# The second expert layer of a perceiver kernel: token and expert pairs sorted into 23 tiles of 128 slots, instead of every expert run over all 1024 tokens

## The reference

```python
probs = softmax(einsum('bsd,ed->bse', x, router_w))
token_probs, probs_idx = top_k(probs, 2)
gates = sum(token_probs[..., None] * one_hot(probs_idx, 8), axis=-2)
# for each expert e:
y = gelu(x @ wg_w[e].T + wg_b[e], approximate=False)     # 256 -> 1024
h = y * (x @ w1_w[e].T + w1_b[e])                        # 256 -> 1024
out = h @ w2_w[e].T + w2_b[e]                            # 1024 -> 256
acc = acc + out * g[..., None]
```

## Time and profile before

| | |
|---|---|
| median of 3 runs | 5568.69 us (5562.72 to 5574.45) |
| profiled execution, its own time | 5562.66 us |
| its span in the trace | 5560.9 us |
| mean granted TensorE clock | 0.912 of full |
| `l1_ffn`, first load to its last DVE instruction | 3040.4 to 3622.4 us |

### The profile page before, as it was taken

How to read it: one execution, slowest core, us unless ns; L and a number is a source line. 1 busy time by engine, 2 the same in 40 slices (tenths; PEclk the granted TensorE clock), 3 DMA queues, 4 the chain that set the end, 5 groups by cost and what they waited for, 6 DMA issues and landing times. The chain is left out here.

```text
span 5560.9 us, 113654 instructions
## 1 busy us (share of the span) xinstructions
PE 4837.1 (87%) x45694; PEld 3720.1 (67%) x45694; DVE 3035.0 (55%) x5687; ACT 2118.8 (38%) x4053; POOL 935.9 (17%) x473
## 2 busy tenths in 40 slices
PE   6879999998759989999766899987689989998877
PEld 4659888896549966666423788876269956665465
DVE  5358777772554455555287433354633366664443
ACT  1235555552134434444243333343034434443121
POOL 0022222220002200000076122142612200000200
PEclk8889999999669999999988899988879999999885
DMA  1010000000101111110022111022911010000110
GB/s 60 29 36 15 15 22 15 16 7 27 50 31 45 45 43 50 38 50 26 22 76 69 46 45 50 18 81 57 121 46 53 23 38 26 27 21 33 42 59 30
DMA packets 195844, 222.91 MB, mean 40 GB/s; under 512 B 43251, under 2 KB 164932, under 8 KB 187236
## 3 DMA queue, kind: packets, MB, share of 16 engines
q1 hardware_dynamic: 195428, 216.93, 13.9%
HBM read 170.09 MB, written 15.34 MB: 33 GB/s over the span
## 5 line engine op out<-in xcount | busy, mean ns | idle before, releaser
L2367 DVE TENSOR_REDUCE block_max<-PS 128x1 f32<-128x512 f32 (+1 forms) x896 | 505.5, 627 | 300.3 <-PE PS L2227 299.7
L2316 ACT ACTIVATE probs_turned<-PS 128x512 f32<-128x512 f32 (+1 forms) x896 | 434.6, 571 | 563.3 <-PE PS L2248 563.2
L1632 PE MATMUL PS<-input_part,part_up 128*128 128x512 f32 x2304 | 552.5, 393 | 18.4 <-DVEq L1713 8.6
L1645 PEld LDWEIGHTS PS<-part_down,hidden_part 128*128 128x128 f32 x4608 | 548.7, 189 | 2.0
L1645 PE MATMUL PS<-part_down,hidden_part 128*128 128x256 f32 x4608 | 549.1, 281 | 0.0
L1685 ACT ACTIVATE hidden<-PS,b 128x512 f32<-128x512 f32 x384 | 264.4, 689 | 651.7 <-PE PS L1632 637.2
L1632 PEld LDWEIGHTS PS<-input_part,part_up 128*128 128x128 f32 x2304 | 434.9, 190 | 110.1 <-DVEq L1713 9.3
L844 PE MATMUL PS<-context_turned,queries 128*128 128x512 f32 x1728 | 413.4, 384 | 25.3 <-issue 18.4
L876 PE MATMUL PS<-probs_turned,context_part 128*128 128x256 f32 (+2 forms) x3120 | 410.1, 286 | 3.7 <-DVE weighted L953 3.7
L905 ACT CAST probs_turned<-PS 128x512 fp32r<-128x512 f32 x576 | 261.2, 510 | 358.3 <-PE PS L856 358.3
L1721 DVE TENSOR_TENSOR hidden_part<-hidden,hidden_part 128x512 fp32r<-128x512 f32 x384 | 293.8, 774 | 183.1 <-ACT hidden_part L1675 182.4
(11 more groups left out here) (441 smaller groups left out, 8052.8 us busy)
## 6 DMA issues: line engine op xcount, KB each, us to landing
context_rows<-in_ctx SPq DMA_DIRECT2D x40, 768.0 KB
raw_up<-in_L_ffn_W SPq DMA_DIRECT2D x16, 1024.0 KB, 4.8
raw_down<-in_L_ffn_W SPq DMA_DIRECT2D x16, 1024.0 KB, 4.8
v_all<-v_turned SPq DMA_DIRECT2D x128, 128.0 KB, 19.4
ctx_turned<-context_turned SPq DMA_DIRECT2D x16, 800.5 KB, 4.7
context_turned<-ctx_turned SPq DMA_DIRECT2D x16, 800.5 KB
b_all<-bc_turned SPq DMA_DIRECT2D x32, 256.0 KB, 3.5
c_all<-bc_turned SPq DMA_DIRECT2D x32, 256.0 KB, 4.3
```

The costliest lines, as they stand in the source:

```text
L1632: last = nc.tensor.matmul(PS[:, k % ring + 2 * x, :], bank.parts[name][a][:, c, f * P:(f + 1) * P], h[b][:, c, half * 512:(half + 1) * 512 ...
L1645: last = nc.tensor.matmul(PS[:, 4 + t % outs, 0:DIM], aT[a][:, f, t * P:(t + 1) * P], bank.parts["down"][b][:, f, :], start=(f == 0 and m ...
L2316: nc.scalar.activation(probs[0:kk, t % ring, i, 0:many].rearrange("p k c s -> p (k c s)"), PS[0:kk, bank_of("turned", t, i), 0:many * 2 * ...
L2367: nc.vector.tensor_reduce(part[:, b % 2, chunks[0]:chunks[-1] + 1, i, u // 2], bank, AX_X, ALU.max).then_inc(max_done.sem, 1)
```

## The change

`l1_ffn` no longer calls `gate_bias` and `experts`, but `routed_experts`. The 1024 tokens have 2048 pairs (token, chosen expert). The pairs of an expert get consecutive slots, and each expert begins at a multiple of 128 slots, so that a tile of 128 slots belongs to one expert; 23 tiles (`SLOTS`) hold any distribution, and all 23 are always computed. DVE works out each pair's slot (`idx`) and each tile's expert (`expert_of`) from `first` and `second`, with two small PE matmuls for the counts. GpSimd scatters the rows of U into a tensor in device memory, `slot_rows`, with 16 indirect transfers of 128 rows, and SP loads all slots back in four batches. For each tile, SP reads the expert's number into a register and loads that expert's three weight tensors (1 MB each) and two columns of biases into one of three buffers. PE turns a tile's rows over, multiplies, and the sums of each tile are stored to `slot_sums` in device memory by ACT's queue. At the end GpSimd gathers the two sums of every token with 16 indirect transfers, and DVE adds them, times the token's two probabilities, to X. The output biases are weighted with the gates as before, but added to X before the tiles. The matmuls are on float32 itself: no operand is split. Before the tiles are scattered, `slot_rows` is filled from the input x (three transfers of 1, 1 and 0.9 MB) so that unused slots hold numbers.

```diff
+SLOTS = 2 * TOKENS // P + EXPERTS - 1
...
+class RoutedExperts:
...
+        self.ring = 3
+        sizes = {"up": [P, self.ring, DC, 4 * DIM], "second": [P, self.ring, DC, 4 * DIM], "down": [P, self.ring, 4 * DC, DIM]}
...
+        self.slot_rows = core.nc.dram_tensor(name, (SLOTS * P, DIM), F32, kind="Internal").ap()
...
+        x, cuts = d["x"], range(0, SLOTS * P, TOKENS)
+        self.loads = [(self.slot_rows[r:min(r + TOKENS, SLOTS * P)], x[0:min(TOKENS, SLOTS * P - r)], self.filled) for r in cuts]
...
+def routed_experts(core, bank, rows, first, second, share, b2, iota, func, skip=None):
...
+    x_bank, y_bank, small_bank = 4, 5, 7
...
+    batches = [range(n, min(n + 6, SLOTS)) for n in range(0, SLOTS, 6)]
...
+                def weights_of(i):
+                    u = i % ring
+                    e = sp.value_load(expert_of[0:1, i:i + 1], min_val=0, max_val=EXPERTS - 1)
+                    if i >= ring:
+                        sp.wait_ge(up_ready.sem, up_ready.at((i - ring + 1) * GROUPS))
+                    for k in up_names:
+                        sp.dma_start(bank.w[k][:, u], bank.source[k][bass.ds(e, 1)].squeeze(0)).then_inc(w_landed[k][u].sem, 16)
+                    if i >= ring:
+                        sp.wait_ge(made.sem, made.at((i - ring + 1) * FC))
+                    for k, src in bank.columns.items():
+                        sp.dma_start(bank.col[k][:, u], src[bass.ds(e, 1)].squeeze(0)).then_inc(c_landed[u].sem, 16)
+                    if i >= ring:
+                        sp.wait_ge(y_ready.sem, y_ready.at(i - ring + 1))
+                    sp.dma_start(bank.w["down"][:, u], bank.source["down"][bass.ds(e, 1)].squeeze(0)).then_inc(w_landed["down"][u].sem, 16)
+                sp.wait_ge(tile_ready.sem, tile_ready.at(1))
+                weights_of(0)
+                sp.wait_ge(scattered.sem, scattered.at(16 * 2 * TILES))
+                for n, some in enumerate(batches):
+                    sp.dma_start(xg[:, some[0]:some[-1] + 1, :],
+                                 bank.slot_rows[some[0] * P:(some[-1] + 1) * P].rearrange("(i p) d -> p i d", p=P)).then_inc(brought[n].sem, 16)
+                for i in range(1, SLOTS):
+                    weights_of(i)
...
+                pool.wait_ge(bank.filled.sem, bank.filled.past)
+                pool.wait_ge(place_ready.sem, place_ready.at(1))
+                for t in range(TILES):
+                    for k in range(2):
+                        nc.gpsimd.indirect_dma_start(bank.slot_rows, bass.IndirectOffsetOnAxis(idx[:, k, t:t + 1], 0), rows[:, t, :],
+                                                     None).then_inc(scattered.sem, 16)
+                for k in range(3):
+                    pool.wait_ge(stored[k].sem, stored[k].at(16 * len(range(k, SLOTS, 3))))
+                for t in range(TILES):
+                    for k in range(2):
+                        nc.gpsimd.indirect_dma_start(yk[:, k, t, :], None, bank.slot_sums,
+                                                     bass.IndirectOffsetOnAxis(idx[:, k, t:t + 1], 0)).then_inc(gathered[t // 2].sem, 16)
...
+                then(v.memset(ones[:], 1.0))
+                then(v.tensor_tensor_scan(below[:], ones[:], core.ident[:], 0.0, ALU.mult, ALU.add))
+                v.tensor_tensor(below[:], below[:], core.ident[:], ALU.subtract).then_inc(ones_made.sem, 1)
+                v.tensor_tensor(both[:], first[:], second[:], ALU.add).then_inc(counted.sem, 1)
...
+                dve.wait_ge(prefix.sem, prefix.at(1))
+                then(v.tensor_copy(tot[:].rearrange("p e t -> p t e"), PS[:, small_bank, 64:128].rearrange("p (t e) -> p t e", e=EXPERTS)))
+                then(v.tensor_tensor_scan(flat(cum), flat(fresh), flat(tot), 0.0, ALU.mult, ALU.add))
...
+                v.tensor_copy(idx[:], at2[:]).then_inc(place_ready.sem, 1)
...
+                v.tensor_copy(expert_of[:], expert[:]).then_inc(tile_ready.sem, 1)
...
+                for n, b in enumerate((2, 3, 5, 6)):
+                    tiles = X[:, 2 * n:2 * n + 2, :]
+                    v.tensor_tensor(tiles, PS[:, b, :].rearrange("p (t d) -> p t d", d=DIM), tiles, ALU.add).then_inc(bias_taken.sem, 1)
...
+                for i in range(SLOTS + 1):
+                    if mult and i < SLOTS:
+                        dve.wait_ge(c_landed[i % ring].sem, c_landed[i % ring].at(16 * len(bank.columns) * (i // ring + 1)))
+                        for f in range(FC):
+                            dve.wait_ge(up_act.sem, up_act.at(i * FC + f + 1))
+                            v.scalar_tensor_tensor(hT[:, i % 2, f, :], PS[:, 2 + f // 4, (f % 4) * P:(f % 4 + 1) * P],
+                                                   bank.col["second"][:, i % ring, f:f + 1], a32[:, i % 2, f, :],
+                                                   ALU.add, ALU.mult).then_inc(h_ready.sem, 1)
+                    if i:
+                        dve.wait_ge(y_ready.sem, y_ready.at(i))
+                        if i > 3:
+                            dve.wait_ge(stored[(i - 1) % 3].sem, stored[(i - 1) % 3].at(16 * ((i - 1) // 3)))
+                        v.tensor_copy(ysb[:, (i - 1) % 3, :], PS[:, y_bank + (i - 1) % 2, 0:DIM]).then_inc(y_moved.sem, 1)
+                dve.wait_ge(bias_taken.sem, bias_taken.at(4))
+                for t in range(TILES):
+                    for k in range(2):
+                        n = t * 2 + k
+                        dve.wait_ge(gathered[t // 2].sem, gathered[t // 2].at(64))
+                        if k:
+                            dve.wait_ge(summed.sem, summed.at(n))
+                        v.scalar_tensor_tensor(X[:, t, :], yk[:, k, t, :], share[:, t, k:k + 1], X[:, t, :],
+                                               ALU.mult, ALU.add).then_inc(summed.sem, 1)
...
+                def turned_out(i):
+                    act.wait_ge(x_ready.sem, x_ready.at(i + 1))
...
+                def sums_out(i):
+                    act.wait_ge(y_moved.sem, y_moved.at(i + 1))
+                    act.dma_start(bank.slot_sums[i * P:(i + 1) * P], ysb[:, i % 3, :]).then_inc(stored[i % 3].sem, 16)
+                turned_out(0)
+                for i in range(SLOTS):
+                    act.wait_ge(c_landed[i % ring].sem, c_landed[i % ring].at(16 * len(bank.columns) * (i // ring + 1)))
+                    if mult and i >= 2:
+                        act.wait_ge(h_ready.sem, h_ready.at((i - 1) * FC))
+                    for f in range(FC):
+                        if f % 4 == 0:
+                            act.wait_ge(up_ready.sem, up_ready.at(i * GROUPS + f // 4 + 1))
+                        nc.scalar.activation(a32[:, i % 2, f, :], PS[:, f // 4, (f % 4) * P:(f % 4 + 1) * P], func,
+                                             bias=bank.col["up"][:, i % ring, f:f + 1]).then_inc(up_act.sem, 1)
+                    if i + 1 < SLOTS:
+                        turned_out(i + 1)
+                    if i >= 2:
+                        sums_out(i - 2)
...
+                last.then_inc(bias_ready.sem, 1)
+                def turned(i):
+                    pe.wait_ge(brought[i // 6].sem, brought[i // 6].at(16))
+                    if i:
+                        pe.wait_ge(x_taken.sem, x_taken.at(DC * i))
+                    for c in range(DC):
+                        last = nc.tensor.transpose(PS[:, x_bank, c * P:(c + 1) * P], xg[:, i, c * P:(c + 1) * P], core.ident[:])
+                    last.then_inc(x_ready.sem, 1)
+                def up(i):
+                    u = i % ring
+                    pe.wait_ge(x_taken.sem, x_taken.at(DC * (i + 1)))
+                    for k in up_names:
+                        pe.wait_ge(w_landed[k][u].sem, w_landed[k][u].at(16 * (i // ring + 1)))
+                    for f in range(FC):
+                        if i and f % 4 == 0:
+                            pe.wait_ge(made.sem, made.at((i - 1) * FC + f + 4))
+                        for x, k in enumerate(up_names):
+                            for c in range(DC):
+                                last = nc.tensor.matmul(PS[:, 2 * x + f // 4, (f % 4) * P:(f % 4 + 1) * P],
+                                                        bank.w[k][:, u, c, f * P:(f + 1) * P], xT[:, i % 2, c, :],
+                                                        start=(c == 0), stop=(c == DC - 1))
+                        if f % 4 == 3:
+                            last.then_inc(up_ready.sem, 1)
+                def down(i):
+                    u = i % ring
+                    pe.wait_ge(w_landed["down"][u].sem, w_landed["down"][u].at(16 * (i // ring + 1)))
+                    pe.wait_ge(made.sem, made.at((i + 1) * FC))
+                    if i >= 2:
+                        pe.wait_ge(y_moved.sem, y_moved.at(i - 1))
+                    for f in range(FC):
+                        last = nc.tensor.matmul(PS[:, y_bank + i % 2, 0:DIM], hT[:, i % 2, f, :], bank.w["down"][:, u, f, :],
```

(36 more changed lines are left out.)

164 lines of the change are left out of this document (added).

## The result

The changed kernel takes 5299.65 us (median of 4 runs, 5285.47 to 5301.34) against 5570.66 us for the kernel before, run beside it (5562.72 to 5574.45): a ratio of 0.951, with a 95% interval of 0.949 to 0.9529.

The account below looks back on a forecast made before the run. TensorE's matmul time was taken to bound the expert loop (busy 532.0 of 533.0 us). Way in, 23 tiles at 11.5 us (265) and way out made 361.6 us instead of 582.0, leaving 5342, plus 6: 5348 us; range 5315 to 5455.

Parts of the forecast that it names:

- two best experts known: Start of the sublayer: 26.6 us less 2 for a dropped bias load the router waited for, 24.6 (bounds 23 and 31).
- 16 scatters and landing: Before the tiles: 16 indirect transfers on GpSimd at 1.5 us each, 24 us, then 2.0 us for the landing.
- lower clock, second tile: Start of the tile loop: PE begins at half clock and the second tile's weights queue behind slot loads, 4 us for both.
- way out: After the tiles: copy, issue and landing, 16 gathers at 1.5 us, landing, last additions: 31 us.
- Of the profiled execution's 5562.7 us 5342 remain: Whole program: the stage's 220 us saving taken off the profiled execution, every other sublayer keeping its time.
- I take 0.119 x 64 = 7.6 us: Up matmuls of a tile: 64 float32 passes of 128 columns at 0.119 us each, 7.6 us.
- four waits of 0.05 us a tile: PE in each tile: four waits already met, estimated at 0.05 us each, 0.2 us together.
- Rival 1: Tile matmuls: weight loads and short float32 streams don't overlap, up to 141 us more, 5489 us; chance 0.07.
- Rival 2: Scatters and gathers: indirect transfers cost nearer 4.86 us each, 107 us more, 5455; chance 0.10 for over 3 us.
- Rival 3: Tile loop: PE's clock stays at 0.50, a tile takes 22.8 us, 259 us more, 5607, slower; chance 0.05.
- Rival 4: GpSimd: each indirect transfer holds the queue until landed, 19.4 us, 573 us more, 5921, slower; chance 0.03.
- The sum by non-overlapping transfers: Scatters and gathers: at the skill's 2.3 us per transfer without overlap, 32 x 0.8 = 26 us higher, 5374 us.

Follow-up runs that it names:

- run 1: The kernel after, again, with no edit: 5302.04 us against 5560.47 for the kernel before, ratio 0.9546; sublayer 335.5 us.
- run 2: The kernel before, again, with no edit: 5568.15 us; sublayer 582.0 us.
- run 5: The kernel after with up matmuls that stream 64 columns instead of 128: sublayer 348.4 us, 12.9 more; a pass still 0.1115 us.
- run 11: The kernel after with half the weight columns in all up matmuls: sublayer 338.4 us, 2.9 more; four passes every 0.437 us.
- run 6: The kernel after with only the first choice's eight gathers and additions at the end: sublayer 324.5 us, 11.0 less; whole 5318.35 us.
- run 3: The kernel after with each weight load moving half its weights, used twice by the matmuls: sublayer 335.5 us, unchanged; whole 5292.99 us.
- run 7: The kernel after with the weights of the first three tiles, not one, issued before SP waits for the scatters: sublayer 344.5 us, 9.0 more.
- run 12: The kernel after with only the first choices' eight scatters: sublayer 328.6 us, 6.9 less.
- run 14: The kernel after with twelve small dependent DVE steps added behind the sublayer: sublayer 338.5 us, 3.0 more; whole 5310.9 us.
- run 4: The kernel after with two buffers for each weight tensor instead of three: sublayer 348.6 us, 13.1 more.
- run 9: The kernel after with half the weight columns in every second group of up matmuls, streams whole: sublayer 396.5 us, 61 more.
- run 10: The kernel after with half the weight columns and half the streamed columns in every second group of up matmuls: sublayer 359.9 us.
- run 13: The kernel after with fifty small dependent DVE steps added behind the sublayer: sublayer 346.2 us, 10.6 more; whole 5341.57 us.

## Why the prediction missed low

Inside the sublayer the mechanism was right: PE's passes set the loop, the transfers are hidden, the ends are GpSimd's. In us of each step:

| step | predicted | measured |
|---|---|---|
| two best experts known | 24.6 | 22.0 |
| slots worked out | 5.7 | 6.0 |
| 16 scatters and landing | 26.0 | 22.6 |
| slot rows, turning, copies | 5.3 | 6.0 |
| lower clock, second tile | 4 | 3.4 |
| 23 tiles | 265 | 248.6 |
| way out | 31 | 27.0 |
| sublayer | 361.6 | 335.5 |

- **The step that put the time outside the range is the sum's last, which keeps all other sublayers at their time: "Of the profiled execution's 5562.7 us 5342 remain".** The time came out 48 us under the forecast. The sublayer's terms are 26 of them, which alone gives 5322, within the range. Another 15 are the profiled difference outside the sublayer, a term put at nothing without a reason. The last 8 are the forecast's 6 us between the median and the profiled execution, and the 1.7 by which the median of the kernel after lay below its own. Runs 1 and 2 show the outside term again: 23 to 27 us behind the sublayer, 12 us net by the medians of run 1.
- **Inside the sublayer the step that failed most is "I take 0.119 x 64 = 7.6 us".** The pass is 0.1115: 0.5 us a tile, 11 us in all. The premise, that passes which load 128 columns of weights "never come closer than 0.12 us", took the length of a row of passes for their distance. By the starts that stand in the same rows, the 24 passes of L876, 128 columns wide and split, fill 3743.90 - 3741.19 = 2.71 us, 0.113 each. Only the passes of 256 columns take 0.119, so the price is not the same at 128 and at 256 columns; why those take 0.119 stays open. Runs 5 and 11 show what holds a pass of 128 columns, 0.1115 by the load and 0.109 by the stream. The same reading made the 0.255 of the 512-column passes: the three groups of rows 3 add up to 574.9 us in a stretch of 533, which is no small overlap. Nothing else hung on that one.
- The four waits of 0.05 us a tile aren't there: PE was busy 241.17 of 241.17 us. 0.2 us a tile, 5 us in all.
- The indirect transfers, a guess between 0.43 and 4.86 us, are 1.26: 32 x 0.24 = 8 us less. Run 6 shows that their issue alone is on the path of the way out. The range's lower end took 0.43 for them and everything else as forecast.
- The router no longer waits for the bias load: 2 us were taken off, 4.6 came. The waits named for it had 3.76 in one piece.
- Outside the sublayer, the executions before and after differ in the granted clock of sublayers that no edit touched. The time behind it was 1908.4, 1915.2 and 1915.1 us in the three executions with the sublayer at 335.5 us (the kernel after, runs 1 and 3), so part of the 271 us seems to belong to this kernel as it stands. Runs 7 and 12 had that gain too, 11 a third less, 5 and 14 about half; 4, 6, 9, 10 and 13 had none of it (1935.5 to 1945.5). These are single executions, and what decides which clock a sublayer gets was not found.

The 10 us between 261 by the profiled executions and 271 by the medians are how far the profiled execution of before lay below its median (8.0) and that of after above it (1.7).

The change does two things at once, and no run separates them: fewer rows, and float32 matmuls of two passes instead of split ones of three. An estimate from passes of this trace: split, a tile of 128 slots would have 96 up passes at 0.113 and 24 down passes at 0.119, 13.9 us with its turning, 71 us more over 23 tiles, besides the work of splitting. By that the sorting alone brings most of the gain, but not all.

**The rivals.** Rival 1 (loads and streams don't overlap) is out for tiles of one width; where the width changes between groups 0.17 us come on top, for a reason that no run shows. The Trainium skill (TensorE: Matmul & The Clock Gate, Step-by-step: what each phase is for) says that the next weights load while the present matmul runs, on a read port of their own. Runs 5 and 11 agree with the overlap, 0.1115 and 0.109 us, where a whole one and half of the other in a row would take 0.16; no run shows the port. The Trainium skill (TensorE: Matmul & The Clock Gate, LDWEIGHTS (loading the stationary operand)) gives a weight load's time as columns divided by 1.2 in ns, by estimate 107 ns for 128. The 0.1115 us of run 5 lie 4% above it. Rival 2 (more than 3 us for an indirect transfer) is out at 1.26. Rival 3 (half clock) is out here, at 1.00 from the second tile on, with the reservation of run 5. Rival 4 is out: a scatter issues every 1.26 us, also in run 7 with the DMA engines full. The sum by non-overlapping transfers, 26 us higher, is out as well: scatters that landed 4.0 us after their issue came 1.26 us apart.

**What was said of the trace.** Clock 1.00 from the second tile, PE at 100% of the loop, DMA share 0.76, no wait for `routed_` tensors: as forecast. The tiles are 10.8 instead of 11.5 us apart. The gap between `place` and the first L2057 was 28.6 us (31 forecast), that from the last L2070 to the next sublayer 27.0 (31).

## What to carry to other kernels

A float32 matmul with 128 streamed columns costs about as much by its weight load (0.1115 us a pass) as by its stream (0.109), so sorting tokens into tiles of 128 loses next to nothing to loads and gains by the rows that it drops; 64 columns gained nothing. Price a pass by the distance of two starts, not by the length of a row of passes. Price the ends of such a routed layer by GpSimd's issue, 1.26 us for 128 rows, and issue no large load shortly before a chain of small transfers that something waits for. When untouched parts of a kernel move by more than a few tenths of a per cent, compare the granted clock and PE's busy time there before crediting the change, judge an edit by the length of its own stretch, and give a forecast's range some room for the rest, here 12 to 25 us.

## What the runs showed of the hardware that was not expected

- A change in the number of weight columns between successive matmuls, 128 to 64 or back, cost 0.17 us each time in run 9 (1.22 us for a pair of groups, where uniform groups make 0.88) and 0.15 in run 11.
- With up matmuls of 64 columns (run 5, one execution) PE, busy 21 of its first 23 us, stayed at 0.50; with 128 columns, in the kernel after, it had 0.85 in the first tile and 1.00 after it.
- The same 608 PE instructions of the last sublayer took 159.4, 162.5 or 171.1 us, at mean granted clocks of 0.63, 0.61 and 0.56, in executions of one and the same kernel too: 159.4 and 162.5 in two of the kernel after.
- An indirect transfer of 128 rows of 1 KB takes GpSimd 0.96 us and 0.30 more to the next, scatter and gather alike.
- Large loads issued just ahead of the scatters, by SP and not by GpSimd, went with a landing of the scatters that was 2.7 to 3.7 us later (runs 12 and 7).
